# Graph attention's epilogue moved into the group loop, with inverse roots on GpSimd

## The reference, cut to what matters

```python
h = relu(layernorm(x))
# attention over edges (dst, src), v = h @ v_w.T + v_b
scores = clip(sum(qk[dst] * qk[src]) / 8, -5, 5)
out = softmax-weighted sum over src of v        # 64 wide
out = out @ o_w.T + o_b
t = out + h
x = x + (layernorm(t) * ln_g + ln_b)            # attention layer's result
z = relu(layernorm(x))                          # input of the GCN
# GCN: deg counts edges into a node (plus itself), dinv = rsqrt(deg)
sum over src of dinv[src] * dinv[dst] * (z @ W)[src], twice
```

## Time and profile before

| | |
|---|---|
| median of 3 executions | 7746.43 us (7723.70 to 7751.26) |
| profiled execution | 7695.61 us, its span 7693.8 us |
| TensorE busy, share of the span | 5787.1 us, 75% |
| VectorE / ScalarE / GpSimd busy | 4073.2 / 2576.5 / 3044.5 us |
| mean granted TensorE clock | 0.869 |

### The profile page before, as it was taken

How to read it: one execution, slowest core, us unless ns; L and a number is a source line. 1 busy time by engine, 2 the same in 40 slices (tenths; PEclk the granted TensorE clock), 3 DMA queues, 4 the chain that set the end, 5 groups by cost and what they waited for, 6 DMA issues and landing times. The chain is left out here.

```text
span 7693.8 us, 170283 instructions
## 1 busy us (share of the span) xinstructions
PE 5787.1 (75%) x40448; PEld 4192.9 (54%) x40449; DVE 4073.2 (53%) x12741; ACT 2576.5 (33%) x4844; POOL 3044.5 (40%) x3157
## 2 busy tenths in 40 slices
PE   4776777777777776577777777777777697999699
PEld 3555555555555555455555555555555583222689
DVE  6454555555555555455555555554555527778532
ACT  2233333333333333333323333332333215777210
POOL 3455555555555553455555555555555000000000
PEclk9888888888888888788888888888888898999899
DMA  3332322232232222332223323322222372323479
GB/s 78 74 77 67 78 77 71 77 79 69 76 77 68 77 72 60 77 79 69 76 69 78 78 69 77 77 71 77 77 70 77 149 274 78 133 104 109 172 296 362
DMA packets 689322, 764.62 MB, mean 99 GB/s; under 512 B 368995, under 2 KB 574026, under 8 KB 664145
## 3 DMA queue, kind: packets, MB, share of 16 engines
q1 hardware_dynamic: 561703, 577.65, 24.3%
q0 software_dynamic: 100352, 102.96, 6.9%
q10 hardware_dynamic: 27180, 82.93, 2.8%
HBM read 671.04 MB, written 88.81 MB: 99 GB/s over the span
## 5 line engine op out<-in xcount | busy, mean ns | idle before, releaser
L336 POOL DMA_INDIRECT gat_rows<-rows_scr,gat_idx x3136 | 3017.7, 962 | 2881.3 <-PE gat_aps L1352 1261.8
L1343 PE MATMUL gat_tps<-ident,gat_weights 128*128 128x128 f32 x3136 | 602.2, 323 | 1356.4 <-ACTq L1208 1237.9
L1343 PEld LDWEIGHTS gat_tps<-ident,gat_weights 128*128 128x128 f32 x3136 | 384.7, 159 | 1544.8 <-ACTq L1208 1372.0
L1225 ACT ACTIVATE adj_tiles<-gat_counts 128x392 f32 (+1 forms) x784 | 390.6, 498 | 2206.4 <-remote 1153.7
L1361 PE MATMUL gat_sps<-gat_relu,gat_att 128*128 128x256 f32 x3136 | 1084.7, 479 | 0.0
L1124 DVE CUSTOM_DVE_ANT_0 gat_masked<-gat_sps,gat_miss,gat_oldtop 128x512 f32<-128x512 f32 x784 | 586.6, 748 | 782.2 <-remote 513.0
L1075 DVE TENSOR_SCALAR adj_hot_key<-adj_iota_key,adj_winbase,adj_key 128x392 bf16<-128x392 int16 x2416 | 962.1, 398 | 7.6 <-issue 7.6
L1352 PE MATMUL gat_aps<-gat_rows,gat_weightsT 128*128 128x65 f32 x6224 | 957.9, 307 | 0.0
L1352 PEld LDWEIGHTS gat_aps<-gat_rows,gat_weightsT 128*128 128x128 f32 x6224 | 940.8, 231 | 0.0
L1116 DVE COPY gat_oldtop<-gat_top 128x1 f32 x784 | 119.8, 153 | 1354.8 <-issue 610.3
L1074 DVE TENSOR_SCALAR adj_hot_lo<-adj_iota_lo,adj_low 128x128 bf16<-128x128 int16 x2416 | 631.8, 261 | 265.3 <-issue 110.8
(11 more groups left out here) (384 smaller groups left out, 6824.3 us busy)
## 6 DMA issues: line engine op xcount, KB each, us to landing
gcn_sum_adj<-adj_scr SPq DMA_DIRECT2D x98, 1568.0 KB, 8.4
gat_dstb<-dst_scr SPq DMA_DIRECT2D x784, 128.0 KB
gat_ea<-in_ea SPq DMA_DIRECT2D x784, 128.0 KB
gin_sum_adj<-adj_scr SPq DMA_DIRECT2D x49, 1568.0 KB, 8.4
adj_scr<-adj_tiles ACTq DMA_DIRECT2D x48, 1568.0 KB
at_adj<-adj_scr SPq DMA_DIRECT2D x60, 1024.0 KB, 9.5
gat_rows<-rows_scr,gat_idx POOLq DMA_INDIRECT x3136
gat_xr<-xr_scr SPq DMA_DIRECT2D x1568, 24.0 KB
```

Of the source, the lines that this page charges most:

```text
L336: pool.indirect_dma_start(ring.rows[:, u, c, 0:ROW], None, rows_d, bass.IndirectOffsetOnAxis(ap=ring.idx[:, u, c:c + 1], axis=0)).then_inc ...
L1343: last = pe.transpose(tps[:, c * P:(c + 1) * P], wts[:, j, c * P:(c + 1) * P], ident[:])
```

## The change

The work of the blocks after attention goes into attention's group loop, and attention's caller no longer calls them. In detail:

- `turn_back` multiplies the sums with `wo`, the output projection stacked twice, in place of `fold`. SyncE loads it and the bias at attention's start; the bias is added to `h` and `ln_b` to `x` there, on VectorE, over all 49 tiles.
- In group g, VectorE does for the four tiles of group g-1: `finish` (now in the block at unit 8), the residual and its centring (unit 12), the variance's sum (unit 16), the norm (unit 20, before `weigh(u + 3)`), the gain and the sum into x. For those of group g-2 it does the second norm's centring (unit 0), the variance's sum (unit 4), the norm with relu and `dinv` folded into the root (unit 8), and the two remainders for the bf16 parts (units 12 and 16).
- ScalarE squares the centred values (at units 12 and 0, the waits on VectorE in its own queue) and writes the three parts (units 12, 16, 20, before `direct`).
- GpSimd makes `dinv` at the start and then, twice per group, an inverse root over [128, 4] from an integer seed and three Newton steps: 14 instructions for the first norm, 15 for the second, a drain behind each.
- The last full group and the single last tile end together: their roots are ScalarE's Sqrt and VectorE's reciprocal.
- The GCN's first `propagate` gets `ready=True`: it makes no parts. Both GCN sums have 192 columns instead of 193, since neither uses the degrees.

The diff, cut to its core:

```diff
-    W = 3 * D + 1
+    W = 3 * D + (deg is not None)
...
-            pe.wait_ge(s_part, 5)
+            if not ready:
+                pe.wait_ge(s_part, 5)
...
-            for level in range(3):
+            for level in range(0 if ready else 3):
...
-def attention(nc, k, adj_d, keys, values, out, ident, ones):
+def attention(nc, k, adj_d, keys, values, ident, ones, h, x, wo_d, ln_g, ln_b, deg, dinv, parts):
...
+            def inverse_root(root, of, t):
+
+                pool.tensor_scalar(root.bitcast(I32), of.bitcast(I32), -0.5, float(SEED), ALU.mult, ALU.add)
+                pool.drain()
+                for _ in range(3):
+                    pool.tensor_tensor(t, root, root, ALU.mult)
+                    pool.drain()
+                    pool.tensor_tensor(t, t, of, ALU.mult)
+                    pool.drain()
+                    pool.tensor_scalar(t, t, -0.5, 1.5, ALU.mult, ALU.add)
+                    pool.drain()
+                    pool.tensor_tensor(root, root, t, ALU.mult)
+                    pool.drain()
+
+            def spread(g, ln, tiles):
+                var, root = st[:, ln, 1, 0:tiles], st[:, ln, 2, 0:tiles]
+                pool.wait_ge(s_var[ln], g + 1)
+                pool.tensor_scalar(var, var, 1.0 / D, EPS, ALU.mult, ALU.add)
+                pool.drain()
+                inverse_root(root, var, trial[:, 0:tiles])
+                if ln == 1:
+                    pool.tensor_tensor(root, root, dinv[:, g * GT:g * GT + tiles], ALU.mult)
+                pool.drain().then_inc(s_root[ln], 1)
+
+            pool.tensor_scalar(deg[:, 0:NT], deg[:, 0:NT], 1.0, None, ALU.add)
+            pool.drain()
+            inverse_root(dinv[:, 0:NT], deg[:, 0:NT], trial[:])
+            for g in range(GROUPS - 1):
+                for ln in range(2):
+                    spread(g, ln, GT)
...
+            for j in range(2):
+                sp.dma_start(wo[j * D:(j + 1) * D, :], wo_d[0:D, :]).then_inc(s_wo, 16)
+            sp.dma_start(bo[:], wo_d[D:D + 1, :].to_broadcast([P, D])).then_inc(s_wo, 16)
...
+            pe.wait_ge(s_wo, 48)
...
-                    pe.matmul(folded[:, a, 0:D], sums[:, at], fold[:], start=True, stop=True)
+                    pe.matmul(folded[:, a, 0:D], sums[:, at], wo[:], start=True, stop=True)
...
+            def square_of(ln, turn, tiles, what):
+                act.wait_ge(s_off[ln], turn)
+                act.activation(square[:, ln, 0:tiles, :], what, ACT.Square).then_inc(s_squared[ln], 1)
+
+            def residual_square(g, tiles=GT):
+                square_of(0, g + 1, tiles, out[:, 0:tiles, :])
+
+            def node_square(g, tiles=GT):
+                square_of(1, g + 1, tiles, h[:, nodes_of(g, tiles), :])
+
+            def root_of(ln, tiles):
+                act.wait_ge(s_last[0], ln + 1)
+                act.activation(st[:, ln, 2, 0:tiles], st[:, ln, 1, 0:tiles], ACT.Sqrt).then_inc(s_last[1], 1)
+
+            def part_of(g, level, tiles=GT):
+                at = nodes_of(g, tiles)
+                act.wait_ge(s_rest[min(level, 1)], (g + 1) * (2 if level else 1) - (level == 1))
+                act.activation(parts[:, at, level * D:(level + 1) * D], left[:, 0:tiles, :] if level else h[:, at, :], ACT.Copy
+                               ).then_inc(s_part, 1)
+
...
-            def group(g, odd, first=False):
+            def group(g, odd, behind=2):
                 for u in range(0, UNITS, 4):
                     low(g, u)
                     low(g, u + 1)
                     late(g, u)
                     low(g, u + 2)
                     late(g, u + 1)
+                    if behind > 1 and u in (12, 16, 20):
+                        part_of(g - 2, u // 4 - 3)
                     direct(g, u + 3)
                     late(g, u + 2)
-                    if u == 4 and not first:
-                        evacuate(g - 1, GT, 1 - odd)
+                    if behind:
+                        if u == 4:
+                            evacuate(g - 1, GT, 1 - odd)
+                        if u == 12:
+                            residual_square(g - 1)
+                    if u == 0 and behind > 1:
+                        node_square(g - 2)
                 direct_end(g, GT)
 
-            group(0, 0, True)
-            with act.Fori(0, GROUPS // 2 - 1) as i:
+            group(0, 0, 0)
+            group(1, 1, 1)
+            with act.Fori(1, GROUPS // 2) as i:
...
+            part_of(GROUPS - 2, 0)
+            residual_square(GROUPS - 1, GT + LAST)
+            part_of(GROUPS - 2, 1)
+            root_of(0, GT + LAST)
+            part_of(GROUPS - 2, 2)
+            node_square(GROUPS - 1, GT + LAST)
+            root_of(1, GT + LAST)
+            for level in range(3):
+                part_of(GROUPS - 1, level, GT + LAST)
...
+            dve.tensor_tensor(x[:], x[:], ln_b[:].unsqueeze(1).to_broadcast([P, NT, D]), ALU.add)
+            dve.wait_ge(s_wo, 48)
+            dve.tensor_tensor(h[:], h[:], bo[:].unsqueeze(1).to_broadcast([P, NT, D]), ALU.add)
...
+            def center(ln, to, what, tiles):
+                mean = stat(ln, 0, tiles)
+                dve.tensor_reduce(mean, what, AX.X, ALU.add)
+                dve.drain()
+                dve.tensor_scalar(mean, mean, 1.0 / D, None, ALU.mult)
+                dve.drain()
+                dve.tensor_tensor(to, what, per_tile(mean, tiles), ALU.subtract).then_inc(s_off[ln], 1)
+
+            def variance(g, ln, tiles=GT):
+                dve.wait_ge(s_squared[ln], g + 1)
+                dve.tensor_reduce(stat(ln, 1, tiles), square[:, ln, 0:tiles, :], AX.X, ALU.add).then_inc(s_var[ln], 1)
+
+            def last_root(ln, tiles):
+                var, root = stat(ln, 1, tiles), stat(ln, 2, tiles)
+                dve.wait_ge(s_squared[ln], GROUPS)
+                dve.tensor_reduce(var, square[:, ln, 0:tiles, :], AX.X, ALU.add)
+                dve.drain()
+                dve.tensor_scalar(var, var, 1.0 / D, EPS, ALU.mult, ALU.add).then_inc(s_last[0], 1)
+                dve.wait_ge(s_last[1], ln + 1)
+                dve.reciprocal(root, root)
+                dve.drain()
+                if ln == 1:
+                    dve.tensor_tensor(root, root, dinv[:, (GROUPS - 1) * GT:NT], ALU.mult)
+                    dve.drain()
+
+            def residual(g, tiles=GT):
+                at = nodes_of(g, tiles)
+                dve.tensor_tensor(out[:, 0:tiles, :], out[:, 0:tiles, :], h[:, at, :], ALU.add)
+                dve.drain()
+
+            def residual_center(g, tiles=GT):
+                center(0, out[:, 0:tiles, :], out[:, 0:tiles, :], tiles)
+
+            def residual_norm(g, tiles=GT):
+                if tiles == GT:
+                    dve.wait_ge(s_root[0], g + 1)
+                dve.tensor_tensor(out[:, 0:tiles, :], out[:, 0:tiles, :], per_tile(stat(0, 2, tiles), tiles), ALU.mult)
+                dve.drain()
+
+            def residual_gain(g, tiles=GT):
+                dve.tensor_tensor(out[:, 0:tiles, :], out[:, 0:tiles, :], ln_g[:].unsqueeze(1).to_broadcast([P, tiles, D]), ALU.mult)
+                dve.drain()
+
+            def node_add(g, tiles=GT):
+                at = nodes_of(g, tiles)
+                dve.tensor_tensor(x[:, at, :], x[:, at, :], out[:, 0:tiles, :], ALU.add)
+                dve.drain()
+
+            def node_center(g, tiles=GT):
+                at = nodes_of(g, tiles)
+                center(1, h[:, at, :], x[:, at, :], tiles)
+
+            def node_norm(g, tiles=GT):
+                at = nodes_of(g, tiles)
+                if tiles == GT:
+                    dve.wait_ge(s_root[1], g + 1)
+                dve.scalar_tensor_tensor(h[:, at, :], h[:, at, :], 0.0, per_tile(stat(1, 2, tiles), tiles), ALU.max, ALU.mult
+                                         ).then_inc(s_rest[0], 1)
+
+            def left_over(g, level, tiles=GT):
+                at = nodes_of(g, tiles)
+                dve.wait_ge(s_part, 3 * g + level + 1)
+                dve.tensor_tensor(left[:, 0:tiles, :], left[:, 0:tiles, :] if level else h[:, at, :],
+                                  parts[:, at, level * D:(level + 1) * D], ALU.subtract).then_inc(s_rest[1], 1)
+
+            def group(g, behind=2):
                 for u in range(0, UNITS, 4):
                     weigh(g, u, GT)
                     if u:
                         join(g, u // 2 - 1)
+                    if u == 4 and behind > 1:
+                        variance(g - 2, 1)
+                    if u == 16 and behind:
+                        variance(g - 1, 0)
                     weigh(g, u + 1, GT)
                     clip(g, u + 3)
+                    if u == 0 and behind > 1:
+                        node_center(g - 2)
+                    if u == 12 and behind:
+                        residual(g - 1)
+                        residual_center(g - 1)
                     weigh(g, u + 2, GT)
                     join(g, u // 2)
+                    if behind > 1:
```

(46 more changed lines are left out.)

89 lines of the change are left out of this document (39 added, 50 removed).

## The result

| | before | changed |
|---|---|---|
| median of 4 executions | 7746.19 us (7723.70 to 7751.26) | 7669.55 us (7649.79 to 7690.92) |
| ratio, 95% interval | | 0.991 (0.988 to 0.994) |
| profiled execution, its span | 7695.6, 7693.8 us | 7690.9, 7689.1 us |

The kernel is 0.9% faster: 70 us by the ratio, 47 to 92 by its interval. On another chip the same pair gave 7605.06 us (6 executions) against 7687.53 (11), ratio 0.990 (0.987 to 0.992).

What follows compares the result with a forecast made beforehand. TensorE bounds attention, a VectorE chain the stretch after it. 58.3 + 1.0 − 1.1 − 10 = 48.2 us off the median of 7746.4 gave 7698 us, range 7668 to 7742.

Steps and rivals of the forecast that it cites:

- the seam: Between attention's last division and the graph sum's first matmul, 79.8 us of mostly VectorE chain: shortened by 58.3 us (55 to 60).
- One column at 2.4 GHz on 2401 matmuls is 1.0 us for each of two sums: Both GCN sums, 192 columns instead of 193: 1.0 us gained in all (0 to 2).
- Each GpSimd step … holds back the next by up to 0.17 … 10 us lost: GpSimd's roots in attention's groups: steps hold up VectorE's instructions, costing 1.0 us per group, 10 us over ten groups.
- The sign to look for, weighings longer than 1.22 in the units 16 to 23: Next profile, attention's groups: VectorE's weighings in these units would exceed 1.22 us if the forecast was right.
- the GpSimd steps of 0.2 to 1.3 us: Next profile, attention's groups: GpSimd's root steps would take 0.2 to 1.3 us, not all 0.17, if the forecast was right.
- (a): Unit 16 of a group: ScalarE's relu waits for VectorE's centring, but ends 0.4 us before score 18 needs it.
- (b): First four units of a group: ScalarE's relu of unit 4 waits for the node's centring, with 0.8 us spare.
- (c): A group's end: the last weighing finishes 1.6 us later, with 1.9 us spare before its value product.
- The start of attention: Three small loads ahead of the asked keys on SP cost 1.1 us (0.9 to 2); VectorE's two added sums stay hidden.
- The roots hide entirely: Rival, GpSimd's roots in the groups: loss only 0 to 5 us, gain 53 to 58, time 7690 us; chance 0.22.
- The roots come late: Rival, groups: GpSimd steps of 1.4 us delay the roots, costing TensorE 95 us in all, time 7785 us; chance 0.08.
- a stall limits itself at 4.5 us a root: Argument against late roots in the groups: while VectorE waits, GpSimd runs unhindered, so a stall stops at 4.5 us per root.

## Why the prediction was right, and where its sum was not

It forecast 7698 us in a range of 7668 to 7742; the median is 7669.55, 1.6 us inside the low end. Faster was right, and the seam, which carries the gain, was right to 1 us. Two smaller terms were wrong, both against the change, by 22 us together, and a third was 3.6 us too low. Of the 28 us under the forecast 20 are these terms and the rest is scatter of the executions. The range held because 27 us of scatter had been added to it, so that it holds is in part luck.

- **The seam: right.** 79.8 to 20.5 us, forecast 58.3 gained, measured 59.3; the first matmul 20.5 us behind the last division, forecast 21.5; released by a load 6.5 us after its issue, forecast 6.3. The chain up to the last part copy took 13.4 us instead of 14.9, the change of block 0.6 instead of 0.35, so the errors are small and in part cancel.
- **"One column at 2.4 GHz on 2401 matmuls is 1.0 us for each of two sums": mis-sized.** The step took a column for its share of a matmul. Measured are 3.1 ns for this column in a full row and not 0.4: 13.4 us for both sums (2.8 ns over all 4802 matmuls), 12.4 more than I counted and outside my bounds of 0 to 2. The earlier trace rows held one width only; a price for one column taken from a single width was not a bound.
- **"Each GpSimd step … holds back the next by up to 0.17 … 10 us lost": refuted as a mechanism.** The period stayed at 59.33. The holds that were tested cost 0.1 us a group. The earlier trace rows shows one long VectorE instruction that waited behind GpSimd's sums, and I read a symmetric exclusion from it. In the loop it is the small GpSimd instructions that wait, for one VectorE instruction or for eight. The sign to look for, weighings longer than 1.22 in the units 16 to 23, did not come; the GpSimd steps of 0.2 to 1.3 us, which I had also named, did (the longest 1.7). The Trainium skill (SBUF — State Buffer, section on the two separate sides) states the lock as one for which the instruction that starts first blocks the other; the trace agrees that they exclude each other (0.20 us of GpSimd's work takes 0.98 to 1.7 beside a weighing), and shows beyond it that an unbroken row of VectorE instructions keeps it for 7.7 us.
- **Places (a), (b), (c): nearly right.** ScalarE waits 1.29 us for the centring at unit 16 (the square at 6822.76) and no score is late. The group's end is weighed at 6847.03, 2.4 us behind the place that it had in the kernel before; I had 1.6 and 3.1 more for GpSimd. It fits in the spare, if barely: two more Newton steps in each root, 2.7 us of GpSimd's own time, cost 5.0 us of TensorE's a group.
- **The start of attention: a little low.** +4.7 us, +3.1 in another execution (60.3), against 1.1 (0.9 to 2). The three issues take the 1.8 us from 6481.31 to 6483.13 on SP, and the first score comes 3.35 us after the asked keys' issue instead of 2.47: 2.7 of the 4.7 us. Of the other 2.0 us, 1.6 are what sets this execution apart from the other one of the same kernel, and they go with the clock, which I had left out here. The first 20 us from the first issue, before, in the changed kernel and in its other execution:

```profile
6418.05:6438.05 20.00, 15.04 (x54) 4.29 (x56) 9.74 (x13) 15.16 (x15) 0.00 (x0) 0.91 0.96 347
6481.31:6501.31 20.00, 12.51 (x36) 3.76 (x36) 13.40 (x11) 11.22 (x11) 10.27 (x14) 0.66 0.82 289
6389.00:6409.00 20.00, 12.16 (x42) 3.74 (x44) 13.41 (x11) 12.11 (x12) 10.28 (x14) 0.83 0.82 288
```

TensorE is idle for the first 5.2 us of the changed kernel's attention instead of 2.5, and the granted clock is 0.66 or 0.83 instead of 0.91. The ten profiles with the loads on SyncE fall in two groups: 61.9 to 62.0 us to the first issue in the loop at a clock of 0.66 (five), and 60.0 to 60.7 at 0.76 to 0.83 (five).
- **The rivals.** "The roots hide entirely" is what happened, for 0.22 of the chance against 0.45 for the forecast itself; the time that it gave, 7690, is 20 high, 12 of them for the column. "The roots come late" did not happen, but the kernel with the norms right behind the sums is that case. My remark that a stall limits itself at 4.5 us a root was about right for a root that VectorE waits for from its start (5.0 and 5.3 there), but it left out what the clock then costs, 5.0 us a group.

With these terms the sum is 59.3 + 13.4 − 4.5 = 68.2 us, and 7746 less 68 is 7678; the measured ratio gives 70 us (47 to 92), the two medians differ by 76.6.

## What to carry to other kernels

Small GpSimd work beside a busy VectorE cost VectorE next to nothing here (0.1 us of 59.3), but how long it takes is VectorE's to decide: 14 steps took some 4.8 us alone (14 × 0.34) and 13.3 beside it. Take its result as far behind as that, not sooner: two results asked for at once cost 11.5 us a group, and two more steps in each root 5.0. Price a stall of TensorE with the clock behind it: of 12.1 us in such a group 5.0 were slower matmuls. Measure the output width of a matmul on both sides of 192 before pricing a column by its share. And when work that used to cover a load is moved away, issue the load earlier too (6.3 us here).

## What the runs showed that I had not expected

- A GpSimd instruction over 128x4 takes 0.20 us and a dependent one follows 0.34 to 0.36 later, behind a drain. Held by VectorE it took up to 7.71.
- Behind 3.67 us of idle TensorE in the middle of attention, eight matmuls that take 1.06 us took 1.94.
- A VectorE loop made longer by drains was faster (64.32 to 62.97 us a group), since the drains let GpSimd in.
- A bf16 matmul with 192 output columns takes 82.4 ns in a full row of 49, with 193, 194 and 200 columns 85.5, 85.1 and 85.7.
- A bias of one row, issued 0.25 us after SyncE began to issue 1 MB loads, held VectorE until 7.0 us after its issue.
